# Decoder layer, fp32: inputs of the cross attention requested at the end of the self-attention block, and the first projection ahead of the key product

## The chip, the cores and the metric

The kernel runs on one core of a Trainium2 chip. The metric is the device time of one execution in microseconds; before the change the median of 3 runs is 1337.78 us (1329.46 to 1340.32). The engines are named as the profile names them: PE (TensorE, matmul; PEld its weight loads), DVE (VectorE), ACT (ScalarE), POOL (GpSimd) and SP (SyncE, which issues most DMAs here; SPq is its queue). Each runs its own instructions in program order and waits on semaphores.

## What is computed

One pre-norm decoder layer on `x` of 4 x 1024 x 256 in fp32: self-attention with rotary embedding (16 heads of 16), cross attention over 4 x 77 context rows (one head of 256), and a mixture of 8 experts in which each expert picks its 512 tokens. Cut to what matters:

```python
# self-attention
out = softmax(rot(q) @ rot(k).T * scale) @ v          # per batch and head
x = x + (out @ proj_w.T + proj_b)
# cross attention, k = v = ctx_1024
kp = ctx @ Wk.T ; vp = ctx @ Wv.T + bv
qp = layernorm(x) @ Wq.T + bq
x = x + softmax(qp @ kp.T / 16) @ vp @ Wo.T + bo
# experts: top-cap tokens of each expert, gelu between two layers, gated, scattered
x = x + moe(layernorm(x))
```

## The kernel before, in words

Four stages follow one another, each in a block of its own with a barrier of all engines between: `project_qkv`, `attend`, `cross_attend`, `experts`. A block's instructions on each engine stand in the order of the code; nothing reorders them.

`attend` runs over 4 batches (`bodies`: first and last written out, the middle ones a loop), 8 half groups each. Each half group ends in a tail that is spread over engines and lies behind in time: ACT copies the sum to `b_out` (L615), SP gathers the denominators into `b_sums` (`Tail.sums`, L432), DVE inverts them (`Tail.invert`, L438), SP stores and spreads the reciprocals (`Tail.spread`, L443 and L446), POOL scales into `b_att` (`Tail.scale`, L454), and SP stores that to `attended` in DRAM (`Tail.store`, L461). `ost` is that DRAM tensor, `s_os` the semaphores of its stores (`b_out_stored`). The very last half group's tail is done within `cross_attend`.

`cross_attend` works on 8 chunks of 512 tokens. For a chunk, SP loads the attention's output (`attT`, tile `c_attT`, 512 KB) and `x` (`xs`, tile `c_x`, 512 KB) in `load(j)`, alternating between two buffers; POOL adds the projection's bias (`bias`, L1043, to `c_xb`); PE multiplies with `wp` (`project(j)`); DVE adds both (`residual`, L1074) and makes mean and variance, ending in `c_nm` (L1132); ACT normalises (`c_xn`, L972); PE transposes (L1231) and multiplies with the folded keys `c_kqw`; softmax; a product with the folded values `c_vo`. Most PE products have one line, L1155, that of the helper `product`. The steps `s` overlap three chunks.

Ahead of the chunks stand products of the context `cT` (tile `c_ctxT`, 308 KB) alone: keys, values, keys folded with `wq`. Their results are taken by ACT (L967, L982). In the queues, at the start of the block: SP issues `cT`, `load(0)`, `load(1)` (five DMAs, 2356 KB), then the last group's `sums` and `spread`, the first expert's weights (2 MB), two constants, the last `store`, and then `load(2)` and on. PE does keys, `project(0)`, values, folded keys, `project(1)`. DVE sets constants, inverts the last sums, and then takes the residual of chunk 0. The buffers of all this are allocated at the block's start, in memory that `attend` has used.

`experts` has two buffers for an expert's output, `yb` (`e_yb`) and `y` (`e_y`).

Of the kernel before, what the change touches and what calls it, by code (L numbers as in the profile page):

```python
# [13 lines left out]
P = 128  # L14
B, L, C = 4, 1024, 256
T = B * L
H, D = 16, 16
SK = 77
E, FF = 8, 1024
CAP = T // E  # L20
KC = C // P
CH = 512
NT = CH // P
G = 4
# [437 lines left out]
                .then_inc(self.s_os[h], 16)  # L462


def attend(nc, ps, ident, group0, s_clear0, stores, last_stores, tail, cw, s_cw, wts, qst, kst, vst):

# [4 lines left out]
    with ctx:  # L471
# [87 lines left out]
        @block.sync  # L559
        def _(sp):  # L560
            def rows(g, h):
                for s, p in ((0, 0), (1, 0), (0, 1), (1, 1)):
                    m = NT * (2 * s + p)
                    for r in range(2):
                        at = HR * s + RS + r
                        sp.dma_start(qs[g][at:at + 1, p, CH * h:CH * h + CH].bitcast(F32),
                                     mT[m:m + NT, r, :].bitcast(F32)).then_inc(s_row[h], 16)

            def ones(g):
                sp.wait_ge(s_clear[g], 4)  # L570
# [12 lines left out]

            def body(i, first, last):
                n = before(i, first)
                for hg in range(NH):
                    back = not (first and hg == 0)
                    m, x = 8 * i + hg - 1, (hg - 1) % 2
                    if back:
                        tail.sums(sp, m, x)  # L590
                    if hg > 1:
                        tail.store(sp, m - 1, i, (hg - 2) // 2, 1 - x)
                    elif not first:
                        tail.store(sp, m - 1, i - 1, NG - 1, 1 - x)
                    if not (last and hg == NH - 1):

                        sp.wait_ge(s_ra, n["rows"] + hg + 1)
                        rows((hg + 1) // 2 % NG, (hg + 1) % 2)
                    if first and hg == 0:
                        last_stores(sp)  # L600
                    if back:
                        tail.spread(sp, m, x)
                    if first and hg == 2:
                        load_context_weights(sp, cw, s_cw, wts)
            bodies(sp, body)
            tail.store(sp, NH * B - 2, B - 1, NG - 1, 0)

        @block.scalar
# [229 lines left out]
            values(B - 1, KT * NH - 1, 1)  # L838


def cross_attend(nc, ps, ident, tail, cw, s_w, ew, s_ew, sums, s_sum, lg, x, ost, wts, out, xrow):

# [5 lines left out]
    with ctx:  # L848
# [6 lines left out]
        SW = SK + E  # L855
        SZ = SK + 2 * E
        ALLK = B * SK
        bqb = sb("c_bqb", [P, KC, P])
        ones = sb("c_ones", [P, P])
        cT = sb("c_ctxT", [P, KC, ALLK])  # L860
        kp = sb("c_kp", [P, KC, ALLK])
        vp = sb("c_vp", [P, KC, ALLK])
        voT = sb("c_voT", [P, KC, ALLK])
# [3 lines left out]
        csum = sb("c_wrn_sums", [P, E])  # L867
        vo = sb("c_vo", [SK, B, C])
        vw = sb("c_vw", [SK, B, E])
        xs = sb("c_x", [P, 2, NT, C])  # L870
        xb = sb("c_xb", [P, 2, NT, C])
        x1 = sb("c_x1", [P, 3, NT, C])
        x2 = sb("c_x2", [P, 2, NT, C])
        xn = sb("c_xn", [P, 2, NT, C])
        z = sb("c_z", [P, 2, NT, C])
        attT = sb("c_attT", [P, 2, KC, CH])
        xnT = sb("c_xnT", [P, KC, CH])
        pT = sb("c_probsT", [SK, CH])
        st = sb("c_st", [P, 2 * NT, 6])
# [14 lines left out]

        s_one = sem("c_ones_set")
        s_set = sem("c_constants_ready")
        s_cx = sem("c_ctx_in")
        s_at = two("c_att_in")
        s_xi = two("c_x_in")
        s_xb = sem("c_x_biased")  # L900
        s_kp, s_kpe = sem("c_k_product"), sem("c_k_taken")
        s_vp, s_vpe = sem("c_v_product"), sem("c_v_taken")
# [21 lines left out]
        def after(eng, s, n):  # L924

            if n > 0:
                eng.wait_ge(s, n)

        @block.sync
        def _(sp):  # L930
            def load(j):
                b, q = j // 2, j % 2
                after(sp, s_m1, 2 * j - 2)
                if j == J - 2:
                    for h in range(2):
                        sp.wait_ge(tail.s_os[h], 16 * G * B * NG)
                sp.dma_start(attT[:, q], ost[b][q].rearrange("k p n -> p k n")).then_inc(s_at[q], 16)
                after(sp, s_xb, j - 1)
                sp.dma_start(xs[:, q], x[b, q].rearrange("t p c -> p t c")).then_inc(s_xi[q], 16)

            sp.dma_start(cT[:], wts["ctxT"]).then_inc(s_cx, 16)
            load(0)
            load(1)
            tail.sums(sp, LAST, 1)
            tail.spread(sp, LAST, 1)
            load_expert(sp, ew, s_ew, wts, 0, 0)
            for n in range(2):
                sp.dma_start(sums[n][:], wts[("blk", "low")[n]]).then_inc(s_sum, 16)
            tail.store(sp, LAST, B - 1, NG - 1, 1)
            for s in range(NS + 1):  # L950
                if s + 2 < J:
                    load(s + 2)
                if 0 <= s - 2 < J:
                    j = s - 2
                    sp.wait_ge(s_m2e, 2 * j + 2)
                    sp.dma_start(out[j // 2, j % 2].rearrange("t p c -> p t c"), x2[:, j % 2]).then_inc(s_so[j % 2], 16)
                if 0 <= s - 3:
                    j = s - 3
                    sp.wait_ge(s_nb, j + 1)
# [190 lines left out]
        def _(pe):  # L1150
# [17 lines left out]
                        last.then_inc(s_m1, 1)  # L1168

            pe.wait_ge(s_w, 12 * 16)  # L1170
            pe.wait_ge(s_cx, 16)
            for e in range(KC):
                product(ps[:, e, 0:ALLK], [(wk[:, k, P * e:P * e + P], cT[:, k, :]) for k in range(KC)]).then_inc(s_kp, 1)
            project(0)
            for e in range(KC):
                product(ps[:, 2 + e, 0:ALLK], [(wv[:, k, P * e:P * e + P], cT[:, k, :]) for k in range(KC)])\
                    .then_inc(s_vp, 1)
# [75 lines left out]
                    project(s + 1)  # L1253


def experts(nc, ps, ident, ew, s_w, sums, s_in, lg, nw, xrow, wts, out):

# [6 lines left out]
    with ctx:  # L1264
# [67 lines left out]
        UP = (3, 4, 7)  # L1332
        NH = 4
        hf = sb("e_hT", [P, NH, CAP])
        yb = sb("e_yb", [P, CT, C])
        y = sb("e_y", [P, CT, C])

        s_z = sem("d_z_ready")
        s_ez = sem("d_exp_ready")
# [499 lines left out]
def program(nc, a, out):  # L1839
# [13 lines left out]
    with ExitStack() as ctx:  # L1853
        hold = lambda n, s, d=F32, c=ctx: c.enter_context(nc.sbuf_tensor(n, s, d))
        signal = lambda n: ctx.enter_context(nc.semaphore(n))
        ps = ctx.enter_context(nc.psum_tensor("banks", [P, 8, 512], F32))

        ident = hold("ident", [P, P])
        cw = {n: hold(f"c_{n}", shapes[n]) for n in CW}
        s_id, s_ld0, s_cw, s_sum = [signal(n) for n in ("ident_in", "group0_loaded", "c_weights_in", "sums_in")]  # L1860
        s_ew = {n: signal(f"e_{n}_in") for n in ("w1", "w2")}
        s_ew.update({n: [signal(f"e_{n}_in{x}") for x in range(2)] for n in ("b1", "b2")})
        tail = Tail(hold, signal, ost, dsum)
        with ExitStack() as early:
            group0 = (hold("b_q0", [P, 2, L], F32R, early), hold("b_k0", [P, 2, L], F32R, early),
                      hold("b_v0", [P, KT, G, VW], F32, early), s_ld0)
            s_clear0 = signal("group0_pad_cleared")
            stores = (hold("a_parts", [P, 4, 2, L], F32R, early), hold("a_v", [P, 2, NT, H, VW], F32, early),
                      [signal(f"a_v_stored{h}") for h in range(2)], [signal(f"a_qk_stored{h}") for h in range(2)])
            last_stores = project_qkv(nc, ps, ident, s_id, group0, s_clear0, stores, x5, a["wqkv"], a["bqkv"], a["cos"], a["sin"], a["ident"],  # L1870
                        qst, kst, vst)
            attend(nc, ps, ident, group0, s_clear0, stores, last_stores, tail, cw, s_cw, a, qst, kst, vst)
        lg = hold("logits", [P, T // P, E])
        sums = [hold(n, [P, P]) for n in ("same_expert", "same_expert_before")]
        ew = {"w1": hold("e_w1", [P, KC, FF]), "w2": hold("e_w2", [P, FF // P, C]),
              "b1": hold("e_b1", [P, 2, FF // P]), "b2": hold("e_b2", [P, 2, C])}
        cross_attend(nc, ps, ident, tail, cw, s_cw, ew, s_ew, sums, s_sum, lg, x5, ost, a, out5, xrow)
        experts(nc, ps, ident, ew, s_ew, sums, s_sum, lg, cw["nw"], xrow.rearrange("b h t p c -> (b h t p) c"), a, out)


# [39 lines left out]
```

## Time and profile before

| | |
|---|---|
| median of 3 runs | 1337.78 us (1329.46 to 1340.32) |
| the profiled execution | 1338.93 us, span 1337.2, mean granted clock 0.91 |
| PE busy | 1133.1 us (85%) |
| DVE busy | 1067.9 us (80%) |
| ACT busy | 762.6 us (57%) |
| POOL busy | 394.9 us (30%) |
| DMA | 120.40 MB, mean 90 GB/s |

The profile shows one execution. A timeline row gives start, duration, engine, line and operation with output<-input, how many such instructions are merged, and in brackets how long the engine sat idle before and what released it. The granted clock is that of TensorE, 1.00 being 2.4 GHz and 0.50 being 1.2 GHz. The cross attention lies between the barriers at about 885.5 and 1031.7 us.

### The profile page before, as it was taken

The page shows a single profiled execution, that of the slowest core. Times are in us where ns is not written, and L with a number is a line of the kernel's source. Part 1 is how long each engine was busy: PE and PEld are TensorE (multiplying, and loading weights), DVE is VectorE, ACT ScalarE, POOL GpSimd, SP SyncE. Part 2 cuts the span into 40 slices and gives each one's busy share as a digit, 9 for nine tenths or more (in the row PEclk, how much of TensorE's full clock was granted, in tenths as well). Part 3 has the DMA queues.
Part 4 walks back from the last instruction along what each step waited for, and adds up shares of the span by engine and source line. Part 5 has one row for each costly group of instructions (what it writes and reads, how often), then busy time and mean ns, then how long its engine had stood idle before and what let it go on. Part 6 is the DMA issues. An engine that isn't in the chain of part 4 may idle for free. (4 is left out here: it accounts for less than half of the span.)

```text
span 1337.2 us, 24904 instructions
## 1 busy us (share of the span) xinstructions
PE 1133.1 (85%) x8470; PEld 613.7 (46%) x8470; DVE 1067.9 (80%) x2458; ACT 762.6 (57%) x929; POOL 394.9 (30%) x396
## 2 busy tenths in 40 slices
PE   5776779899999999899999999988874027999994
PEld 3444433333333333333333333347764026878894
DVE  6776479799999999899999999626875977677751
ACT  2322105687778888778887888843553003466561
POOL 4665684202121121202212000022100021665663
PEclk9989767999999999999999999988885557999997
DMA  3344854644431344324433100035522011354332
GB/s 104 142 172 174 205 158 99 151 102 81 77 72 40 59 82 78 55 40 78 81 75 62 35 15 18 15 91 184 173 79 83 0 63 48 99 156 125 106 96 27
DMA packets 84105, 120.40 MB, mean 90 GB/s; under 512 B 23248, under 2 KB 57040, under 8 KB 82960
## 3 DMA queue, kind: packets, MB, share of 16 engines
q1 hardware_dynamic: 68000, 78.98, 19.6%
q0 software_dynamic: 15984, 39.86, 15.9%
q8 instruction: 69, 1.13, 0.4%
q14 instruction: 52, 0.43, 0.1%
HBM read 75.67 MB, written 42.21 MB: 88 GB/s over the span
## 5 line engine op out<-in xcount | busy, mean ns | idle before, releaser
L686 DVE TENSOR_REDUCE b_max_halves<-banks 128x1 f32<-128x512 f32 x1024 | 628.2, 680 | 27.3 <-PE banks L753 26.9
L628 ACT ACTIVATE b_probs<-banks 128x1024 f32<-128x1024 f32 x512 | 519.9, 1025 | 144.2 <-PE banks L805 142.7
L753 PE MATMUL banks<-b_k,b_q 62*128 62x512 f32 x1024 | 399.2, 472 | 4.8 <-DVE b_max L703 3.1
L805 PE MATMUL banks<-b_q,b_k 64*128 64x512 f32 x1024 | 388.4, 458 | 12.9 <-DMA b_q<-b_max_rows 6.5
L775 PE MATMUL banks<-b_probs,b_v 128*32 128x256 f32 (+1 forms) x3840 | 321.4, 407 | 2.3 <-ACT b_out L615 0.3
L805 PEld LDWEIGHTS banks<-b_q,b_k 64*128 64x128 f32 x1024 | 160.9, 186 | 229.7 <-issue 153.7
L753 PEld LDWEIGHTS banks<-b_k,b_q 62*128 62x128 f32 x1024 | 166.3, 191 | 38.3 <-DVE b_max_halves L686 33.2
L775 PEld LDWEIGHTS banks<-b_probs,b_v 128*32 128x32 f32 x3840 | 75.9, 108 | 166.0 <-issue 85.8
L454 POOL TENSOR_TENSOR b_att<-b_out,b_rec_spread 128x512 f32<-128x512 f32 x32 | 41.1, 1284 | 309.8 <-DMA b_rec_spread<-reciprocals 309.6
L386 POOL DMA_DIRECT2D b_q<-q_stacks x60 | 31.7, 531 | 252.4 <-PE banks L775 232.6
L337 PE MATMUL banks<-a_w,a_xnT 128*128 128x512 f32 x128 | 73.0, 700 | 37.5 <-DVE a_v L266 36.2
L1467 POOL DMA_INDIRECT e_x<-rows,d_idx x32 | 43.9, 1372 | 130.0 <-DVE d_wx L1648 66.2
L1440 ACT ACTIVATE e_hTh<-banks,e_b 128x512 fp32r<-128x512 f32 x64 | 44.1, 689 | 54.0 <-PE banks L1783 51.2
L1684 DVE TENSOR_TENSOR e_hTl<-e_hT,e_hTh 128x512 fp32r<-128x512 f32 x64 | 43.5, 689 | 38.5 <-ACT e_hT L1443 38.5
L1783 PE MATMUL banks<-e_w2h,e_hTh 128*128 128x256 f32 x256 | 73.9, 289 | 0.0
L1783 PE MATMUL banks<-e_w2l,e_hTh 128*128 128x256 f32 x256 | 73.1, 286 | 0.0
L1783 PE MATMUL banks<-e_w2h,e_hTl 128*128 128x256 f32 x256 | 73.1, 285 | 0.0
L314 POOL TENSOR_TENSOR a_t<-a_qk,a_sin 128x256 f32<-128x256 f32 x64 | 52.8, 845 | 66.6 <-DVE a_t L269 66.6
L1426 ACT ACTIVATE e_xTh<-banks 128x512 fp32r<-128x512 f32 x16 | 8.7, 595 | 98.5 <-PE banks L1771 98.5
L217 ACT ACTIVATE a_parts<-banks 128x512 fp32r<-128x512 f32 x32 | 18.9, 592 | 75.7 <-PE banks L350 72.4
L1783 PE MATMUL banks<-e_xTh,e_w1h 128*128 128x512 f32 x128 | 54.0, 422 | 2.6 <-DVE e_xTl L1661 2.6
L1486 POOL DMA_INDIRECT out_x<-e_y,d_idx x32 | 52.2, 1631 | 8.6 <-issue 7.3
(230 smaller groups left out, 1542.6 us busy)
## 6 DMA issues: line engine op xcount, KB each, us to landing
e_w<-in_w SPq DMA_DIRECT2D x16, 1024.0 KB, 10.2
v_tiles<-a_v SPq DMA_DIRECT2D x8, 1024.0 KB, 8.3
q_stacks<-a_parts SPq DMA_DIRECT2D x32, 256.0 KB
k_stacks<-a_parts SPq DMA_DIRECT2D x32, 256.0 KB
b_q<-q_stacks POOLq DMA_DIRECT2D x30, 256.0 KB, 6.5
b_k<-k_stacks POOLq DMA_DIRECT2D x30, 256.0 KB, 7.3
b_v<-v_tiles POOLq DMA_DIRECT2D x15, 512.0 KB, 9.2
a_x<-in_x SPq DMA_DIRECT2D x8, 512.0 KB, 5.9
```

The source lines that it names most:

```text
L314: ins = g.tensor_tensor(dst[:, :, :, u], src[:, :, :, 1 - u], ss, ALU.mult)
L337: mm(ps[:, 2 + q, :], xnT[:, c % 2, k, P * t:P * t + P], w[:, k, 0:2 * C], start=(k == 0), stop=(k == KC - 1))
L628: nc.scalar.activation(pr[:, S % NP, u], ps[:, 2 * u:2 * u + 2, :], ACT.Exp, scale=D ** -0.5).then_inc(s_ex[u], 1)
L686: v.tensor_reduce(mxp[:, (k // NB) % 2, s, p, t, kh:kh + 1], ps[:, bank(last), :], AX.X, ALU.max)\
L753: nc.tensor.matmul(ps[:, bank(last), :], qs[g][stack, p, at:at + P], ks[g][stack, p, CH * kh:CH * kh + CH], start=True, stop=True).then_in ...
L775: last = nc.tensor.matmul(ps[VW * j:VW * j + VW, PV, at], vs[hg // 2][:, kt, j, :], pr[:, S % NP, j // 2, j % 2, at], start=(kt == 0), sto ...
L805: return nc.tensor.matmul(ps[:, 2 * u + s, :], ks[g][stack, u, P * kt:P * kt + P], qs[g][stack, u, CH * h:CH * h + CH], start=True, stop=True)
L1440: nc.scalar.activation(hh[:, f, :], ps[:, UP[f % len(UP)], :], ACT.Gelu, bias=b1[:, x, f:f + 1])
L1467: g.indirect_dma_start(xe[:, x, h, :], None, xrow, bass.IndirectOffsetOnAxis(ap=idx[:, n, h:h + 1], axis=0)).then_inc(s_g[x], 16)
L1486: g.indirect_dma_start(out, bass.IndirectOffsetOnAxis(ap=idx[:, n, h:h + 1], axis=0), y[:, h, :], None, compute_op=ALU.add).then_inc(s_sc, 16)
L1684: v.tensor_tensor(hl[:, f, :], hf[:, f % NH, :], hh[:, f, :], ALU.subtract).then_inc(s_hl, 1)
L1783: ins = mm(o, a, b, start=(start and m == 0), stop=(stop and m == len(pairs) - 1))
```

## The change

The buffers `cT`, `attT` and `xs` and their semaphores move into a class `Firsts`, whose memory is kept from before the attention to the end. The five DMAs (context, chunks 0 and 1) are issued by SP at the end of `attend`, behind the last spread and ahead of the last store of that block, after a wait for batch 0's stores. In `cross_attend` PE does `project(0)` ahead of the keys' product and waits for the context between them. `experts` uses the two halves of `xs` as `yb` and `y`.

```diff
+class Firsts:
+    def __init__(self, sb, sem):
+        self.cT = sb("c_ctxT", [P, KC, B * SK])
+        self.attT = sb("c_attT", [P, 2, KC, CH])
+        self.xs = sb("c_x", [P, 2, NT, C])
+        self.s_cx = sem("c_ctx_in")
...
+    def att(self, sp, ost, j):
+        sp.dma_start(self.attT[:, j % 2], ost[j // 2][j % 2].rearrange("k p n -> p k n")).then_inc(self.s_at[j % 2], 16)
+    def rows(self, sp, x, j):
+        sp.dma_start(self.xs[:, j % 2], x[j // 2, j % 2].rearrange("t p c -> p t c")).then_inc(self.s_xi[j % 2], 16)
...
             bodies(sp, body)
+            for h in range(2):
+                sp.wait_ge(tail.s_os[h], 16 * G * NG)
+            sp.dma_start(firsts.cT[:], wts["ctxT"]).then_inc(firsts.s_cx, 16)
+            for j in range(2):
+                firsts.att(sp, ost, j)
+                firsts.rows(sp, x, j)
             tail.store(sp, NH * B - 2, B - 1, NG - 1, 0)
...
             def load(j):
-                b, q = j // 2, j % 2
-                after(sp, s_m1, 2 * j - 2)
+                sp.wait_ge(s_m1, 2 * j - 2)
                 if j == J - 2:
                     for h in range(2):
                         sp.wait_ge(tail.s_os[h], 16 * G * B * NG)
-                sp.dma_start(attT[:, q], ost[b][q].rearrange("k p n -> p k n")).then_inc(s_at[q], 16)
-                after(sp, s_xb, j - 1)
-                sp.dma_start(xs[:, q], x[b, q].rearrange("t p c -> p t c")).then_inc(s_xi[q], 16)
-
-            sp.dma_start(cT[:], wts["ctxT"]).then_inc(s_cx, 16)
-            load(0)
-            load(1)
+                firsts.att(sp, ost, j)
+                sp.wait_ge(s_xb, j - 1)
+                firsts.rows(sp, x, j)
+
             tail.sums(sp, LAST, 1)
...
             pe.wait_ge(s_w, 12 * 16)
+            project(0)
             pe.wait_ge(s_cx, 16)
             for e in range(KC):
                 product(ps[:, e, 0:ALLK], [(wk[:, k, P * e:P * e + P], cT[:, k, :]) for k in range(KC)]).then_inc(s_kp, 1)
-            project(0)
...
-        yb = sb("e_yb", [P, CT, C])
-        y = sb("e_y", [P, CT, C])
+        yb, y = pair[:, 0], pair[:, 1]
```

On SP, from the last spread of the attention on, the rows before are these (`b_att_ready` is POOL's scaling, the branches the change of block, L929 the start of `cross_attend`):

```order
L446 DMA b_rec_spread<-reciprocals 16x512 [waits b_rec_stored]
L446 DMA b_rec_spread<-reciprocals 16x512 x3
L461 DMA attended<-b_att 16x512 [waits b_att_ready]
L461 DMA attended<-b_att 16x512 x3
L471 UNCONDITIONAL_BRANCH
L929 UNCONDITIONAL_BRANCH [waits barrier_Pool_Activation_PE_DVE_SP_release]
L941 DMA c_ctxT<-in_ctxT 128x616
L937 DMA c_attT<-attended 128x2x512
L939 DMA c_x<-in_x 128x4x256
L937 DMA c_attT<-attended 128x2x512
L939 DMA c_x<-in_x 128x4x256
L432 DMA b_sums<-b_out 32x1x16 [waits b_out_taken]
```

And with the change (L626, L477 and L480 are the loads, L948 the start of `cross_attend`):

```order
L446 DMA b_rec_spread<-reciprocals 16x512 [waits b_rec_stored]
L446 DMA b_rec_spread<-reciprocals 16x512 x3
L626 DMA c_ctxT<-in_ctxT 128x616 [waits b_out_stored1,b_out_stored0]
L477 DMA c_attT<-attended 128x2x512
L480 DMA c_x<-in_x 128x4x256
L477 DMA c_attT<-attended 128x2x512
L480 DMA c_x<-in_x 128x4x256
L461 DMA attended<-b_att 16x512 [waits b_att_ready]
L461 DMA attended<-b_att 16x512 x3
L489 UNCONDITIONAL_BRANCH
L948 UNCONDITIONAL_BRANCH [waits barrier_Pool_Activation_PE_DVE_SP_release]
L432 DMA b_sums<-b_out 32x1x16 [waits b_out_taken]
```

The five loads have moved from behind the barrier to ahead of it and of the last store; `b_sums` is now the first DMA of the block. The 8 DMAs behind it keep their order.

On PE, at the start of `cross_attend`, before (two passes of fp32 appear as one instruction here and as two in the trace):

```order
L1149 UNCONDITIONAL_BRANCH [waits barrier_Pool_Activation_PE_DVE_SP_release]
L1155 MATMUL banks<-c_ctxT,c_wk 128x308 [waits c_ctx_in,c_weights_in]
L1155 MATMUL banks<-c_ctxT,c_wk 128x308 x3
L1155 MATMUL banks<-c_wp,c_attT 128x256 [waits c_att_in0]
L1155 MATMUL banks<-c_wp,c_attT 128x256 x7
L1155 MATMUL banks<-c_ctxT,c_wv 128x308 x4
L1155 MATMUL banks<-c_kp,c_wq 128x308 [waits c_k_taken]
```

With the change:

```order
L1164 UNCONDITIONAL_BRANCH [waits barrier_Pool_Activation_PE_DVE_SP_release]
L1170 MATMUL banks<-c_wp,c_attT 128x256 [waits c_att_in0,c_weights_in]
L1170 MATMUL banks<-c_wp,c_attT 128x256 x7
L1170 MATMUL banks<-c_ctxT,c_wk 128x308 [waits c_ctx_in]
L1170 MATMUL banks<-c_ctxT,c_wk 128x308 x3
L1170 MATMUL banks<-c_ctxT,c_wv 128x308 x4
L1170 MATMUL banks<-c_kp,c_wq 128x308 [waits c_k_taken]
```

The 8 products with `c_attT` have moved ahead of the 4 with `c_wk`; the rest stays.

## Rows read from the trace of the kernel before

**Rows 1.** Chain of waits in order of time, first piece: start us, us, what

```profile
1032.60 0.24 DVE d_io L1503
```

**Rows 2.** Timeline around the barrier, SP and ACT: start us, us, engine line op

```profile
875.47 1.70 SPq L446 DMA_DIRECT2D b_rec_spread<-reciprocals  x4
...
880.04 1.71 SPq L461 DMA_DIRECT2D attended<-b_att  x4
...
882.92 0.60 ACT L615 ACTIVATE b_out<-banks 128x512 f32<-128x512 f32 x1 [1.27 <-PE banks L775]
...
885.48 0.36 SPq L941 DMA_DIRECT2D c_ctxT<-in_ctxT  x1
...
887.94 2.86 SPq L432 DMA_DIRECT2D b_sums<-b_out  x4
```

**Rows 3.** Windows: length, busy us (x) of PE PEld DVE ACT POOL, clock, DMA share, GB/s

```profile
882.86:885.48 2.62, 0.00 (x1) 0.00 (x0) 0.00 (x0) 0.60 (x1) 0.00 (x0) 1.00 0.00 0
885.48:888.64 3.16, 0.00 (x0) 0.03 (x1) 1.25 (x8) 0.00 (x0) 0.21 (x1) 0.50 0.67 192
888.64:892.60 3.96, 3.96 (x9) 2.68 (x10) 0.00 (x0) 0.43 (x1) 0.42 (x1) 0.54 0.99 338
892.60:896.05 3.45, 3.45 (x17) 3.04 (x16) 0.00 (x0) 0.43 (x1) 1.94 (x1) 1.00 0.45 143
896.05:905.30 9.25, 9.25 (x41) 7.10 (x39) 6.91 (x25) 3.94 (x10) 3.63 (x2) 1.00 0.29 66
```

**Rows 4.** Timeline of the cross attention's start, all engines

```profile
888.64 4.12 PE L1155 MATMUL banks<-c_ctxT,c_wk 128*128 128x308 f32 x8 [5.78 <-DMA c_ctxT<-in_ctxT]
...
896.12 2.36 POOL L1043 TENSOR_TENSOR c_xb<-c_x,c_bp 128x1024 f32<-128x1024 f32 x1 [1.58 <-DMA c_x<-in_x]
...
896.94 0.25 DVE L438 RECIPROCAL b_rec<-b_sums 128x16 f32<-128x16 f32 x1 [10.01 <-DMA b_sums<-b_out]
...
897.11 1.22 DVE L1074 TENSOR_TENSOR c_x<-banks,c_xb 128x512 f32<-128x512 f32 x2
...
902.10 0.17 ACT L967 ACTIVATE c_wrn_sums<-banks 128x8 f32<-128x8 f32 x1
...
903.55 0.16 DVE L1132 SCALAR_TENSOR_TENSOR c_nm<-c_mv,c_rs 128x4 f32<-128x4 f32 x1
...
905.87 1.09 PE L1231 MATMUL banks<-ident,c_xn 128*128 128x128 f32 x8 [0.58 <-ACT c_xn L972]
```

**Rows 5.** Timeline of SP: last store of the attention, load of chunk 2

```profile
904.67 2.74 SPq L461 DMA_DIRECT2D attended<-b_att  x4
...
907.46 0.42 SPq L937 DMA_DIRECT2D c_attT<-attended  x1
```

**Rows 6.** Timeline of the step of chunks 1 and 2

```profile
915.35 2.35 POOL L1043 TENSOR_TENSOR c_xb<-c_x,c_bp 128x1024 f32<-128x1024 f32 x1 [11.86 <-DMA c_x<-in_x]
...
918.00 2.34 POOL L1043 TENSOR_TENSOR c_xb<-c_x,c_bp 128x1024 f32<-128x1024 f32 x1 [0.31 <-DMA c_x<-in_x]
...
918.14 2.23 DVE L67 TENSOR_TENSOR c_tm<-c_tm,c_rs 128x4 f32<-128x4 f32 x1
...
920.14 1.99 PE L1155 MATMUL banks<-c_vo,c_probsT 77*128 77x256 f32 x8 [0.68 <-ACT c_probsT L967]
...
920.79 2.08 ACT L972 ACTIVATE c_xn<-c_x,c_nm,c_rs 128x256 f32<-128x256 f32 x4 [0.70 <-DVE c_nm L1132]
...
922.92 1.92 PE L1231 MATMUL banks<-ident,c_xn 128*128 128x128 f32 x8 [0.79 <-ACT c_xn L972]
```

**Rows 7.** Window of the last steps, at the low clock

```profile
998.10:1031.76 33.66, 18.10 (x64) 15.48 (x64) 17.01 (x67) 11.36 (x25) 0.00 (x0) 0.50 0.23 79
```

**Rows 8.** Timeline of DVE, ends of three steps (`c_nm`)

```profile
988.50 0.17 DVE L1132 SCALAR_TENSOR_TENSOR c_nm<-c_mv,c_rs 128x8 f32<-128x8 f32 x1
...
999.94 0.17 DVE L1132 SCALAR_TENSOR_TENSOR c_nm<-c_mv,c_rs 128x8 f32<-128x8 f32 x1
...
1015.93 0.16 DVE L1132 SCALAR_TENSOR_TENSOR c_nm<-c_mv,c_rs 128x4 f32<-128x4 f32 x1
```

More of the change, by code:

```diff
@@ L462, in store, with attend @@
                 .then_inc(self.s_os[h], 16)
-def attend(nc, ps, ident, group0, s_clear0, stores, last_stores, tail, cw, s_cw, wts, qst, kst, vst):
+class Firsts:
[4 more added lines that the diff above has]
+        self.s_cx = sem("c_ctx_in")
+        self.s_at = [sem(f"c_att_in{n}") for n in range(2)]
+        self.s_xi = [sem(f"c_x_in{n}") for n in range(2)]
+    def att(self, sp, ost, j):
+        sp.dma_start(self.attT[:, j % 2], ost[j // 2][j % 2].rearrange("k p n -> p k n")).then_inc(self.s_at[j % 2], 16)
+    def rows(self, sp, x, j):
+        sp.dma_start(self.xs[:, j % 2], x[j // 2, j % 2].rearrange("t p c -> p t c")).then_inc(self.s_xi[j % 2], 16)
+def attend(nc, ps, ident, group0, s_clear0, stores, last_stores, tail, firsts, cw, s_cw, x, ost, wts, qst, kst, vst):
     ctx = ExitStack()
@@ L838, in _, with cross_attend @@
             values(B - 1, KT * NH - 1, 1)
-def cross_attend(nc, ps, ident, tail, cw, s_w, ew, s_ew, sums, s_sum, lg, x, ost, wts, out, xrow):
+def cross_attend(nc, ps, ident, tail, firsts, cw, s_w, ew, s_ew, sums, s_sum, lg, x, ost, wts, out, xrow):
     ctx = ExitStack()
@@ L857, in cross_attend @@
         ALLK = B * SK
+        cT, attT, xs, s_cx, s_at, s_xi = firsts.cT, firsts.attT, firsts.xs, firsts.s_cx, firsts.s_at, firsts.s_xi
         bqb = sb("c_bqb", [P, KC, P])
         ones = sb("c_ones", [P, P])
-        cT = sb("c_ctxT", [P, KC, ALLK])
         kp = sb("c_kp", [P, KC, ALLK])
@@ L869, in cross_attend @@
         vw = sb("c_vw", [SK, B, E])
-        xs = sb("c_x", [P, 2, NT, C])
         xb = sb("c_xb", [P, 2, NT, C])
@@ L875, in cross_attend @@
         z = sb("c_z", [P, 2, NT, C])
-        attT = sb("c_attT", [P, 2, KC, CH])
         xnT = sb("c_xnT", [P, KC, CH])
@@ L896, in cross_attend @@
         s_set = sem("c_constants_ready")
-        s_cx = sem("c_ctx_in")
-        s_at = two("c_att_in")
-        s_xi = two("c_x_in")
         s_xb = sem("c_x_biased")
@@ L1253, in _, with experts @@
                     project(s + 1)
-def experts(nc, ps, ident, ew, s_w, sums, s_in, lg, nw, xrow, wts, out):
+def experts(nc, ps, ident, ew, s_w, sums, s_in, lg, nw, pair, xrow, wts, out):
     ctx = ExitStack()
@@ L1863, in program @@
         tail = Tail(hold, signal, ost, dsum)
+        firsts = Firsts(hold, signal)
         with ExitStack() as early:
@@ L1871, in program @@
                         qst, kst, vst)
-            attend(nc, ps, ident, group0, s_clear0, stores, last_stores, tail, cw, s_cw, a, qst, kst, vst)
+            attend(nc, ps, ident, group0, s_clear0, stores, last_stores, tail, firsts, cw, s_cw, x5, ost, a, qst, kst, vst)
         lg = hold("logits", [P, T // P, E])
@@ L1876, in program @@
               "b1": hold("e_b1", [P, 2, FF // P]), "b2": hold("e_b2", [P, 2, C])}
-        cross_attend(nc, ps, ident, tail, cw, s_cw, ew, s_ew, sums, s_sum, lg, x5, ost, a, out5, xrow)
-        experts(nc, ps, ident, ew, s_ew, sums, s_sum, lg, cw["nw"], xrow.rearrange("b h t p c -> (b h t p) c"), a, out)
+        cross_attend(nc, ps, ident, tail, firsts, cw, s_cw, ew, s_ew, sums, s_sum, lg, x5, ost, a, out5, xrow)
+        experts(nc, ps, ident, ew, s_ew, sums, s_sum, lg, cw["nw"], firsts.xs, xrow.rearrange("b h t p c -> (b h t p) c"), a, out)
 def kernel(**inputs):
```

## The prediction

> **What bounds the kernel now.** I read the chain of waits first. It is followed back from the last instruction and begins at 1032.60 us [rows 1], in the experts' stage; the barrier ahead of that stage cuts it. So the chain says nothing of the cross attention, and what the change is worth must be read from that stage's own timeline. The stages are serial: a barrier at 885.48 us lets the cross attention begin, and the next stage begins when it is over. Whatever the cross attention gains up to its last step comes off the span one for one.
>
> Next the timeline around the barrier. ACT takes the last attention output at 882.92 to 883.52, the last work ahead of the barrier, and SP's first load is issued at 885.48 [rows 2]. The reader sees all inputs of the new stage being asked for only then: five loads, then the tiny `b_sums` transfers behind them at 887.94. TensorE waits 5.78 us with nothing to do (from 882.86) until `c_ctxT` lands at 888.64, the last of the five loads lets POOL begin only at 896.12, and the sums land at 896.94 [rows 4]. VectorE can't add its first residual before that, since `tail.invert` stands ahead of it in its queue.
>
> Last the windows. The granted clock fell to 0.50 (1.2 GHz) during that idle time, stayed there from 885.48 on, and rose to 1.00 (2.4 GHz) during the context's product: 3.96 us at a mean of 0.54 [rows 3]. From 888.64 to 905.30 TensorE is busy without a gap (3.96, 3.45 and 9.25 us, busy throughout) [rows 3]. Then it waits for `c_xn`, which ACT normalises in 2.08 us (as at 920.79 [rows 6]) after `c_nm` at 903.55, and the first transposes start at 905.87 [rows 4].
>
> **The change part by part.**
>
> *The five loads, from 885.48 to the end of the attention.* SP is free after the four `b_rec_spread` transfers (875.47 + 1.70 = 877.17). Its next instruction waits for POOL's `b_att` and is issued at 880.04 [rows 2]. The five issues took 887.94 - 885.48 = 2.46 us before, so they now run from about 877.25 to 879.7, inside that wait. The added wait on `b_out_stored` asks for batch 0 alone, which was stored hundreds of us before. Queued behind the five are only the four stores of `attended` and the barrier. The stores took 1.71 us; behind a full queue the like stores at 904.67 took 2.74 [rows 5]. Even so SP is done at 880.04 + 2.74 = 882.8, ahead of ACT's 883.52. Cost: nothing, with 0.7 us of cover. The last of five loads was usable 896.12 - 885.48 = 10.64 us after the first issue, so now at about 887.9, and the first projection's input, with 820 of the 2356 KB that the five move, at about 882 (an estimate by share of bytes, from the same 10.6 us).
>
> *The last group's sums.* They are now the first thing SP issues in the new stage: 885.5, and 2.86 us for four issues [rows 2]. They landed 0.8 us after the last load before; now the last load is there at 887.9, the last sum about 889. So `b_rec` comes near 889.1, not 896.94, and all that SP does behind it (spread, expert weights, the last store, the load of chunk 2) moves up by about 7.5 us. VectorE's residual is then held by the projection alone.
>
> *The order on TensorE.* `project(0)` goes ahead of the keys. Its data is there when the barrier opens, and I take 885.65 for its start, 0.17 us behind SP's first (an estimate; no row shows TensorE unhindered there). The gapless work until the first transposes stays the same: context 3.96 x 0.54 = 2.14 us at the full clock, then 3.45 and 9.25, together 14.84 us [rows 3]. What it loses in clock must be added. Before, the low level went on for about 3.6 us after TensorE had restarted (3.96 us at a mean of 0.54: 3.6 at 0.50 and the rest at 1.00). I take the same after the new restart: 3.6 us at half speed lose 1.8. So TensorE is through at 885.65 + 14.84 + 1.8 = 902.3. Bounds: no fall of the clock, 900.5; low until 892.1, when it rose before (888.64 + 3.6 rounded down), 903.7.
>
> *Are the transposes then held by something else?* `project(0)` ends at 885.65 + 3.45 + 1.8 = 890.9, the residual follows it, and residual to `c_nm` was 903.55 - 897.11 = 6.44 us: 897.3. ACT has its copies ahead of `c_xn` in its queue; the last ended at 902.27 [rows 4], with the second projection of 3.7 us still to run on TensorE until 905.30, so 3.0 us ahead of TensorE's end; now 899.3, and `c_xn` at 899.3 + 2.1 = 901.4. TensorE is the last at 902.3, by 0.9. POOL's two bias additions of 2.36 us now stand from 885.7 to 890.5, beside VectorE's constants; if they hold VectorE until 890.5, the residual still waits for nothing else. First transposes: 905.87 becomes 902.35, a **gain of 3.5 us**, of the 5.78 that TensorE waited. The rest of that wait is not given back, because the barrier's own 2.8 us remain and ACT's and TensorE's chain is dense.
>
> *Chunks 2 and 3.* Before, `attT` of chunk 2 was issued at 907.46, behind 2 MB of expert weights, and its `c_x` reached POOL at 915.35; POOL ran both bias additions from 915.35 to 920.34 [rows 5, 6]. Beside them VectorE's L67 on 128 x 4 numbers took 2.23 [rows 6], where `c_nm`, of the same size, took 0.16 [rows 4], and `c_nm` of chunk 1 waited for it; ACT began `c_xn` at 920.79 and the transposes waited until 922.92. Now the load is issued near 900 and lands near 907.5, so POOL is through by 912.3, in a time when VectorE waits for ACT's exponentials. `c_nm` comes 2 us earlier, but TensorE had its products with `c_vo` until 922.13 (920.14 + 1.99) [rows 6], so only about **0.7 us** reach the path. The Trainium skill (GPSIMD Engine Reference, 1. Specifications) says that GpSimd's memory interfaces are shared with VectorE, with contention for operations that have two inputs in SBUF; L67 is one, and the row agrees. By that rule alone 2 us would be gained; the sum goes by the rows of TensorE.
>
> *The experts' `e_yb` and `e_y`* lie in the memory of `c_x`, same shapes, freed long before: nothing. From step 2 on each chunk's loads are released by the projections, and the steps hang on one another through the engines.
>
> Sum: 3.5 + 0.7 = 4.2 us. The profiled execution took 1338.93 (span 1337.2 and 1.7 around it), so 1334.7; the median of the runs is 1337.78, 1.15 less, which gives **1333.6 us**.
>
> **Rivals.**
> - *The start stays fast* (no fall of the clock, as the gap is now about 2.8 us and not 5.78). For it: the clock was still at 1.00 for all of 882.86 to 885.48 [rows 3]. Against: it fell just there. Gain 5.3 + 0.7 = 6.0: 1331.8.
> - *The later clock.* The stage goes by the clock: the step from 988.50 to 999.94 took 11.4 us, the next, at 0.50, 16.0 with less work in it, and from 998.10 on all is at 0.50, with 18.10 us of TensorE work [rows 7, 8]. Shifting the stage's gaps by 4 us may move the falls. In favour: one or two steps fast that were slow, 4.5 to 9 us more, 1324.6 to 1329. Nothing in the trace says which way.
> - *The other side, by the same mechanism:* two more steps fall to the low level, 2 x 4.5 = 9 us lost against 4.2 gained: 1342.6, slower than before. It decides from one such step on.
> - *SP is held at the attention's end.* The four stores stand behind 2.36 MB. The Trainium skill (DMA: Bandwidth & Descriptors, Queues, rings and completion order) says that an engine's DMAs go through its own rings in order. If the stores' issue waited for the loads to drain, until 887.9, SP would reach the barrier at 889.6, and the stage would begin some 4.8 us later, all its inputs there: 1338.4. Against it: the stores at 904.67 lost only 1.0 us behind 2 MB [rows 5]; it decides when SP loses over 0.7 us, and cancels the gain from 4.9.
> - *The loads don't come early*, because they share the engines with the attention's last transfers: gain 1 to 2 us, 1336. Against: from 882.86 to the barrier nothing at all was moved [rows 3].
>
> **How the numbers follow.** As summed 0.50; fast start 0.12; later clock in favour 0.15; against 0.10; SP held 0.05; loads late 0.08. The prediction is the likeliest, 1333.6. The runs of before lie 10.9 us apart (1329.46 to 1340.32), so a median of some runs may be off by 3. The likeliest case alone reaches from 1330 to 1337; with the clock's cases the range is 1327 to 1340. About 1% (13 us) is what a measurement of this kernel can tell from no change: faster by more needs the best clock pattern and a low median, 0.08; slower by more 0.03; within 1% 0.89.
>
> **What the profile would show.** Right: the five loads issued from 877 to 880 and the barrier still at about 885.5 (relative to the last `b_out`); TensorE's first matmul with `c_wp` within 0.3 us of it, at clock 0.50 for 3 to 4 us; `b_rec` near 889; first transposes 3.5 us nearer to the barrier; POOL's bias additions for chunks 2 and 3 some 8 us earlier, and no 2 us operation on VectorE. Wrong: a barrier that comes later after ACT's last take; `b_rec` later than 891; the first transposes waiting for ACT; or steps of 14 to 16 us where there were 11.4, which would be the clock.

## The result

| | before | changed |
|---|---|---|
| median (runs) | 1334.55 us (20) | 1327.36 us (20) |
| lowest to highest | 1328.66 to 1344.09 | 1319.33 to 1332.55 |
| ratio | | 0.9942, 95% interval 0.9923 to 0.9961 |
| profiled execution, span | 1337.2 us | 1322.4 us |
| barrier to barrier, cross attention | 146.3 us | 133.3 us |
| experts | 305.4 us | 306.7 us |

The change makes the kernel faster by 0.58% (7.2 us by the medians; 0.39% to 0.77%), so within 1%, as forecast to be likeliest; the forecast size was 4.2 us. With more runs the median of before stands at 1334.55 and not 1337.78. The two profiled executions lie 14.8 us apart. That is more than the medians do: 3.1 us of it are ahead of the barrier (it came at 882.37 and not 885.48), where only the issue of the loads was added; in the profiles below the barrier came anywhere from 882.4 to 885.9, with and without that.

The end of the attention and the start of the cross attention in the changed kernel, from the timeline (as [rows 2, 4, 5]; L626, L477 and L480 are the loads, L1170 is the helper `product`, L1058 POOL's bias, L1089 the residual, L1147 `c_nm`, L1246 the transposes):

```profile
874.27 0.36 SPq L626 DMA_DIRECT2D c_ctxT<-in_ctxT  x1
...
876.22 0.47 SPq L480 DMA_DIRECT2D c_x<-in_x  x1
...
876.91 2.31 SPq L461 DMA_DIRECT2D attended<-b_att  x4
...
879.35 0.60 ACT L639 ACTIVATE b_out<-banks 128x512 f32<-128x512 f32 x1 [1.27 <-PE banks L799]
...
882.37 2.81 SPq L432 DMA_DIRECT2D b_sums<-b_out  x4
...
882.54 4.67 POOL L1058 TENSOR_TENSOR c_xb<-c_x,c_bp 128x1024 f32<-128x1024 f32 x2
...
882.56 5.09 PE L1170 MATMUL banks<-c_wp,c_attT 128*128 128x256 f32 x16 [3.26 <-PEq L489]
...
882.83 2.09 DVE L1075 TENSOR_SCALAR c_wrn<-c_wr,c_nw 128x8 f32<-128x8 f32 x1
...
884.84 2.40 DVE L1075 TENSOR_SCALAR c_wrn<-c_wr,c_nw 128x8 f32<-128x8 f32 x1
...
887.49 2.24 PE L1170 MATMUL banks<-c_ctxT,c_wk 128*128 128x308 f32 x8
...
887.89 0.25 DVE L438 RECIPROCAL b_rec<-b_sums 128x16 f32<-128x16 f32 x1
...
888.06 1.22 DVE L1089 TENSOR_TENSOR c_x<-banks,c_xb 128x512 f32<-128x512 f32 x2
...
894.62 0.17 DVE L1147 SCALAR_TENSOR_TENSOR c_nm<-c_mv,c_rs 128x4 f32<-128x4 f32 x1
...
895.67 2.07 ACT L987 ACTIVATE c_xn<-c_x,c_nm,c_rs 128x256 f32<-128x256 f32 x4
...
898.64 1.04 PE L1246 MATMUL banks<-ident,c_xn 128*128 128x128 f32 x8
...
898.82 0.43 SPq L477 DMA_DIRECT2D c_attT<-attended  x1
```

The five loads go out between 874.27 and 876.69, the barrier opens 2.42 us behind ACT's end (882.37 behind 879.95; before 1.97, and 1.84 to 2.52 in the profiles of all kernels below, with early loads or without), and TensorE starts 0.19 us behind it. `b_rec` is there 5.5 us behind the barrier (11.5 before), the first transposes come at 16.27 us (20.39 before). VectorE's two tiny constants (L1075) take 2.09 and 2.40 us instead of 0.22 beside POOL's bias additions; TensorE's own work still ended last ahead of the first transposes, which show no wait.

The windows of the two profiles, counted from the barrier, show what the prediction had left to chance: the clock of the later steps. In each pair the first window is 15 to 95 us behind the barrier, the second the rest of the stage; the columns are as in [rows 3]. The changed kernel:

```profile
897.37:977.37 80.00, 68.17 (x407) 57.22 (x405) 65.32 (x234) 39.80 (x90) 14.12 (x6) 0.98 0.47 160
977.37:1015.71 38.34, 20.11 (x80) 17.34 (x80) 20.71 (x89) 14.54 (x33) 0.00 (x1) 0.55 0.29 96
```

The same two of a second profile of the kernel before (e_before, below):

```profile
898.87:978.87 80.00, 69.45 (x356) 59.42 (x355) 60.99 (x204) 34.58 (x79) 15.41 (x7) 0.85 0.48 157
978.87:1029.54 50.67, 31.17 (x149) 26.72 (x148) 30.81 (x128) 22.17 (x49) 0.00 (x0) 0.67 0.28 94
```

The column to read is the clock: 0.98 against 0.85 in 80 us. The low level (0.50) held for 3 us in the one and for 24 us in the other ((1 - 0.85) / 0.5 x 80). "Fall" below is a change from 1.00 to 0.50.

### The profile page after: what moved, and what is told of

It is laid out like the page before. It is cut to its first block and busy times, and to the rows that moved or that the text cites. A ratio compares the mean times of both kernels' runs of the same rounds, so it can differ in the third digit from the quotient of the medians.

```text
span 1322.4 us, 24905 instructions
## 1 busy us (share of the span) xinstructions
PE 1129.7 (85%) x8470; PEld 608.6 (46%) x8470; DVE 1069.6 (81%) x2458; ACT 763.1 (58%) x929; POOL 394.5 (30%) x396
## 5 line engine op out<-in xcount | busy, mean ns | idle before, releaser
L829 PE MATMUL banks<-b_q,b_k 64*128 64x512 f32 x1024 | 389.0, 458 | 11.5 <-DMA b_q<-b_max_rows 5.1
L1500 POOL DMA_INDIRECT out_x<-c_x,d_idx x32 | 52.2, 1631 | 8.6 <-issue 7.3
```

Source lines behind the costliest of these rows:

```text
L829: return nc.tensor.matmul(ps[:, 2 * u + s, :], ks[g][stack, u, P * kt:P * kt + P], qs[g][stack, u, CH * h:CH * h + CH], start=True, stop=True)
L1500: g.indirect_dma_start(out, bass.IndirectOffsetOnAxis(ap=idx[:, n, h:h + 1], axis=0), y[:, h, :], None, compute_op=ALU.add).then_inc(s_sc, 16)
```

## The experiments

All ratios are to runs of the kernel before on the same chip, beside the variant's own; they needn't be the quotient of the two medians. In the table, "transposes" is the start of the first transposes of `c_xn` behind the barrier, "steps" the sum of the six distances between `c_nm` of chunk 1 and the sixth `c_nm` after it, "clock" the mean granted clock from 15 to 95 us, all from one profile each. A "filler" is a product whose result nobody uses.

| kernel | median us | ratio (95%) | stage | transposes | steps | clock |
|---|---|---|---|---|---|---|
| before (first profile) | 1334.55 | 1 | 146.3 | 20.4 | 79.3 | 0.85 |
| e_before | 1335.79 | 1.0000 (0.9972 to 1.0028) | 145.7 | 19.9 | 79.3 | 0.85 |
| changed | 1327.36 | 0.9942 (0.9923 to 0.9961) | 133.3 | 16.3 | 72.0 | 0.98 |
| e_after | 1329.59 | 0.9959 (0.9932 to 0.9986) | 131.6 | 17.9 | 71.6 | 1.00 |
| e_keep | 1334.29 | 0.9991 (0.9963 to 1.0019) | 140.5 | 19.5 | 74.9 | 0.91 |
| e_loads | 1327.95 | 0.9942 (0.9916 to 0.9968) | 133.4 | 16.4 | 72.5 | 0.98 |
| e_order | 1329.20 | 0.9957 (0.9933 to 0.9982) | 135.3 | 21.7 | 71.4 | 1.00 |
| e_order_plain | 1327.82 | 0.9951 (0.9927 to 0.9974) | 135.8 | 22.0 | 70.9 | 1.00 |
| e_sums_first | 1334.97 | 1.0004 (0.9977 to 1.0030) | 143.9 | 22.6 | 76.9 | 0.91 |
| e_shift1 | 1332.84 | 0.9981 (0.9954 to 1.0007) | 146.1 | 21.2 | 79.2 | 0.85 |
| e_shift3 | 1335.99 | 1.0020 (0.9995 to 1.0045) | 138.1 | 22.6 | 71.6 | 1.00 |
| e_tail | 1324.38 | 0.9940 (0.9916 to 0.9965) | 134.8 | 16.6 | 77.5 | 0.89 |
| e_warm_before | 1320.76 | 0.9921 (0.9894 to 0.9947) | 130.2 | 20.9 | 69.5 | 1.00 |
| e_warm_order | 1324.02 | 0.9919 (0.9888 to 0.9950) | 132.6 | 22.0 | 70.6 | 1.00 |
| e_warm_after | 1317.96 | 0.9881 (0.9851 to 0.9910) | 125.4 | 16.4 | 71.1 | 1.00 |
| e_warm_loads | 1316.60 | 0.9859 (0.9828 to 0.9890) | 125.7 | 16.5 | 71.3 | 1.00 |
| e_best | 1317.04 | 0.9873 (0.9843 to 0.9903) | 125.3 | 16.4 | 71.0 | 1.00 |

**The change taken apart.** e_after is the changed kernel itself; e_keep undoes both moves and leaves the buffers; e_loads and e_order each undo one.

> The changed kernel again, beside the variants. Its stage (from the barrier to the next one) was 133.3 us against 146.3 before; 4.1 us of that stood at the first transposes, 5.0 at the second, and the other 8 came later, in steps of 11.4 to 12.7 us where there were 12.7 to 14.1. Theory A (a mechanical gain of about 5 us; the rest is the clock's pattern of that one execution): ratio to before 0.994 to 0.997, first transposes again 16.3 us behind the barrier, while the low-clock time ahead of the last 32 us of the stage differs from the 7.8 us of the first profile. Theory B (the change itself keeps the later clock up): the stage is again about 133 us, with under 12 us of low clock ahead of its last 32 us.

> The changed kernel with both moves undone: the loads are issued at the start of the cross attention and the keys' product comes first; only the buffers kept across the stages and the experts' two outputs in the memory of c_x remain. Theory A: no different from before, ratio 0.998 to 1.002, first transposes about 20.4 us behind the barrier, b_rec 11.5 us behind it. Rival C (part of the gain is the placing of the buffers): faster than before by 2 us or more, ratio under 0.9985, in the experts' stage or from step 2 on.

e_loads, the early loads with the old order on TensorE:

```diff
             pe.wait_ge(s_w, 12 * 16)
-            project(0)
             pe.wait_ge(s_cx, 16)
             for e in range(KC):
                 product(ps[:, e, 0:ALLK], ...).then_inc(s_kp, 1)
+            project(0)
```

> The changed kernel with the keys' product ahead of the first projection, as before: the early loads alone. Theory A: TensorE starts at the barrier in either order and does the same work, so first transposes at 16.3 to 16.8 us and a time within 1 us of the changed kernel (ratio to before 0.994 to 0.997). Rival D (the order matters): the first residual is 2 us later, ACT's normalising ends the wait, and over 1.5 us of the gain are lost.

e_order, the loads back in the cross attention (e_keep has both edits):

```diff
-            for h in range(2):
-                sp.wait_ge(tail.s_os[h], 16 * G * NG)
-            sp.dma_start(firsts.cT[:], wts["ctxT"]).then_inc(firsts.s_cx, 16)
-            for j in range(2):
-                firsts.att(sp, ost, j)
-                firsts.rows(sp, x, j)
...
+            sp.dma_start(cT[:], wts["ctxT"]).then_inc(s_cx, 16)
+            for j in range(2):
+                firsts.att(sp, ost, j)
+                firsts.rows(sp, x, j)
             tail.sums(sp, LAST, 1)
```

> The changed kernel with the five loads issued at the start of the cross attention, as before, and the first projection ahead of the keys: the order alone. Theory A: TensorE waits for 820 KB and not for 308, starts 1.5 to 2.5 us later than before, and first transposes come at about 22 us; time 1 to 2 us above before (ratio 1.000 to 1.002). Rival D: the earlier residual brings 1 to 2 us (ratio 0.9985 to 0.9995).

Rival C falls: the placing of the buffers is worth nothing that can be measured (0.9991, 0.9963 to 1.0019). Theory A holds for the loads: with the old order their first transposes come at 16.4 us, as with the new one, and rival D falls. But it is wrong of the order. Alone it was expected 1 to 2 us slower, and its start is slower (transposes at 21.7), yet the kernel gains 0.43%. The profile has the gain in the steps, 71.4 us for six instead of 74.9 to 79.3, at a clock of 1.00. Theory B gets support: the changed kernel's later steps have the high clock in both of its profiles, and so has e_loads without the order (0.98). But e_keep, whose order of instructions is that of before, shows 0.91 and not 0.85, so one profile of a kernel is a weak witness of its clock.

**The clock held up by fillers.** To have the clock alike in all, products whose results nobody uses are put where TensorE waits for the softmax:

```diff
+            def warm(n):
+                for _ in range(n):
+                    mm(ps[:, 6, 384:512], ident[:], ident[:], start=True, stop=True)
             for s in range(NS):
                 if 0 <= s - 2 < J:
+                    after(pe, s_sce, s - 1)
+                    warm(3 if s < J else 14)
                     pe.wait_ge(s_pn, s - 1)
```

> The kernel before with filler products on TensorE while it waits for the softmax: three of 128 columns (about 0.5 to 0.9 us) ahead of the transposes of c_probs in steps with a projection, fourteen in the last two steps, into unused columns of a bank. Their results are not used. Theory A (what the change brings beyond 5 us is fewer falls of the clock in the later steps): the fillers close most of the waits of 1.6 us ahead of which the clock fell, low-clock time ahead of the last 32 us of the stage goes below 12 us from 32, the steps after the third are 11.4 to 12.3 us, and the kernel gains 5 us or more of its own, 1 to 4 more from the last two steps. Theory B (the falls don't come from these waits): the clock falls as before, and the fillers cost 0 to 4 us.

> The changed kernel with the same fillers. Theory A: with the clock alike in both, its distance to the filled kernel before is the mechanical gain alone, 4 to 5 us; the gain over the plain changed kernel is smaller than the fillers bring to the kernel before. Theory B: the distance stays 7 us or more.

The windows of the filled kernel before, and of the filled changed kernel:

```profile
897.43:977.43 80.00, 70.88 (x440) 61.03 (x439) 65.25 (x241) 40.15 (x92) 15.40 (x7) 1.00 0.51 171
977.43:1012.64 35.21, 21.68 (x159) 19.41 (x158) 24.11 (x97) 16.90 (x37) 0.00 (x1) 0.86 0.31 105
```

```profile
900.42:980.42 80.00, 71.35 (x454) 61.91 (x452) 65.63 (x245) 41.24 (x94) 14.10 (x6) 1.00 0.47 164
980.42:1010.80 30.38, 17.25 (x129) 15.56 (x128) 19.41 (x79) 13.27 (x30) 0.00 (x1) 0.85 0.32 107
```

Both stand at 1.00 for the 80 us and at 0.86 and 0.85 after, where before stood at 0.67. The kernel before gains 0.79% (0.53% to 1.06%) from fillers alone. The edit only adds work and a wait, and what the profile shows in return is the clock, so the low level in this stage costs the kernel before some 10 us on the mean (7 to 14 by the interval). Its 6 runs lie within 5.1 us (1319.79 to 1324.91), where the 20 of the plain one spread over 15; six runs spread less than twenty, and the 6 of e_warm_after spread over 8.0.

The first transposes of the filled kernel before, and of the filled changed kernel:

```profile
903.29 1.09 PE L1238 MATMUL banks<-ident,c_xn 128*128 128x128 f32 x8 [0.62 <-ACT c_xn L972]
```

```profile
901.85 1.04 PE L1253 MATMUL banks<-ident,c_xn 128*128 128x128 f32 x8
```

The profiled stages of the two differ by 130.21 - 125.38 = 4.8 us, of which 4.4 stand at these first transposes (20.86 and 16.43 us behind the barrier). **That is the mechanical gain**, what the change brings at an equal clock, and theory A's 4 to 5. The times agree with it but do not fix its size: the ratios differ by 0.9921 - 0.9881 = 0.0040, 5.3 us of 1334, the means of the same runs by 4.7 us (1321.65 and 1316.98) and their medians by 2.8, with six runs each and intervals that overlap.

e_warm_loads and e_warm_order take that gain apart:

> The early loads alone with the fillers. If the loads are the whole mechanical gain: stage 125.0 to 126.5 us, ratio 0.987 to 0.990, no different from the filled changed kernel. If the order has a share: over 1 us longer than that one.

> The order alone (loads late) with the fillers in all steps, so that the clock is alike. Theory A: against the filled kernel before (ratio 0.9921) it is 1 to 2 us slower, ratio 0.992 to 0.994, stage 131 to 132.5 us against 130.2. Rival G: it keeps its 5 us and comes to 0.988 to 0.990.

All of it is the loads'. The filled early loads alone (stage 125.7) are no different from the filled change (125.4), and with the fillers the order alone has nothing left: ratio 0.9919 beside 0.9921, a stage 2.4 us longer. So far as six runs can tell, what it gained in the plain kernel was clock.

**Does the order keep the clock up, or chance?** Two kernels shift the later steps without the order, by six or thirteen fillers ahead of the first transposes:

```diff
                     if j == 0:
                         pe.wait_ge(s_kqe, KC + 1)
+                        warm(6)
```

> The kernel before with six filler products (about 1.3 us) on TensorE ahead of the first transposes, and nothing else: all later steps stand 1.3 us later in the stage, as they do with the order alone. Theory F (the later steps' waits lie otherwise against the moments at which the clock is decided, and that shift gives the order alone its gain): faster than before although it only adds work, ratio 0.995 to 0.998, with one fall or none between 15 and 95 us of the stage. Rival G (the order of the products itself keeps the clock up): 1 to 2 us slower, ratio 1.000 to 1.002, with two or three falls.

> The same with thirteen fillers, about 2.9 us. Theory F: a time that does not follow the added work; somewhere between 4 us faster and 5 us slower than before, with another set of falls. Rival G: 2.5 to 3.5 us slower than before.

> The order alone again, now in the kernel before with its own buffers (no memory kept across the stages). Rival G (the order of the products keeps the clock up): ratio 0.994 to 0.997 as with the kept buffers (0.9957), at most one fall between 15 and 95 us of the stage. Theory H (the 5 us of the order alone were a matter of where the clock's moments lay in those executions): ratio 0.998 to 1.002, with one to three falls.

> The kernel before, unchanged, for a second look into its stage. Ratio 0.998 to 1.002. If falls in the later steps are the rule for it, two or three between 15 and 95 us of the stage, 20 us or more of low clock ahead of its last 32 us; if they are chance, another number than the three of the first profile.

The order's gain came again with the old buffers (0.9951; it was 0.9957 with the kept ones). The first row is the start of e_order_plain, where TensorE waits 7.10 us for the attention's output instead of 5.78 for the context; the second its 80 us:

```profile
888.24 6.59 PE L1155 MATMUL banks<-c_wp,c_attT 128*128 128x256 f32 x16 [7.10 <-DMA c_attT<-attended]
```

```profile
898.78:978.78 80.00, 68.61 (x409) 57.30 (x407) 63.34 (x233) 40.17 (x92) 15.39 (x7) 1.00 0.52 170
```

The second profile of before repeats the first nearly to the tenth: six steps in 79.3 us, clock 0.85. With two gains of the order that stand clear of 1, over 12 runs each, theory H (chance) falls for that gain.

The granted clock of every run, averaged over its whole span, says more than one profile each. Over the 98 runs of before that stood beside the experiments it goes with the time (correlation -0.81): the fastest quarter had 0.913 and 1329.8 us on the mean, the slowest 0.904 and 1339.6. By kernel, the mean is 0.909 for before, e_keep and e_sums_first, 0.913 for the changed kernel's 20 runs, 0.912 for e_after's 12 and 0.9125 for e_loads, and 0.914 and 0.913 for the order alone (e_order and e_order_plain). Up to a third of the changed kernel's rise is its shorter low stretch at the start. And the profiled executions are no fair sample: the two of the changed kernel (1324.07, 1323.94) lie 3.3 and 5.7 us below the medians of their kernels' runs, those of before (1338.93, 1337.31) 4.4 and 1.5 above. Their 3 and 0 us of low clock against 24 overstate the difference.

Theory F (a mere shift by 1.3 us does it) is left open. The profile of e_shift1 shows 0.85 again, and the interval of its 0.9981 includes 1. But over the runs the clock rose with the shifts too, to 0.912 (e_shift1) and 0.911 (e_shift3) from 0.9085 beside them, and e_shift1 was not slower for its added work. The profile of e_shift3 (1.00) is that of its shortest run; its 1.0020 includes 1. What in the order keeps the clock from falling stays open as well. Of the 17 falls between 15 and 95 us in all profiles, 14 came on the heels of two waits of TensorE close together, one of 1.0 to 1.8 us for the probabilities and one of 0.7 us for their transposes; yet in e_after and e_order the same two (1.4 to 1.5 and 0.7 us) passed without a fall. The last two steps have a wait of 3.6 to 3.9 us each, and there it fell in every kernel without fillers in those steps.

**The sums.** e_sums_first issues them ahead of the loads, in the kernel before:

```diff
+            tail.sums(sp, LAST, 1)
             sp.dma_start(cT[:], wts["ctxT"]).then_inc(s_cx, 16)
             load(0)
             load(1)
-            tail.sums(sp, LAST, 1)
```

> The kernel before with one move: the last group's sums are issued ahead of the five loads, all still in the cross attention. b_rec then comes at about 4 us behind the barrier, not 11.5, and the chain behind it on SP (expert weights, chunk 2) is earlier by up to 5 us, with the loads 2.9 us later. Theory A: TensorE's first product waits for the context 2.9 us longer, so first transposes at 22.5 to 23.5 us against 20.4; 1 to 3 us slower than before unless the clock gives some back. Rival E (the sums were what held the start): faster than before by 2 us or more.

Its start, from the timeline:

```profile
885.84 0.22 DVE L1060 TENSOR_SCALAR c_wrn<-c_wr,c_nw 128x8 f32<-128x8 f32 x1
...
888.97 0.25 DVE L438 RECIPROCAL b_rec<-b_sums 128x16 f32<-128x16 f32 x1 [2.16 <-DMA b_sums<-b_out]
...
891.18 4.40 PE L1155 MATMUL banks<-c_ctxT,c_wk 128*128 128x308 f32 x8 [8.77 <-DMA c_ctxT<-in_ctxT]
...
897.41 0.69 DVE L1074 TENSOR_TENSOR c_x<-banks,c_xb 128x512 f32<-128x512 f32 x1 [8.19 <-PE banks L1155]
```

`b_rec` is there 3.6 us behind the barrier, the context at 5.8, and the residual waits for TensorE (8.19 us). The first transposes come at 22.6 us as expected. Rival E falls: the sums alone did not hold the start. The time is that of before; the 2.2 us lost at the first transposes can't be told in it.

**Towards a better version.** e_tail has the fourteen fillers in the last two steps of the changed kernel alone; e_best has all fillers and three more behind the attention's last product.

> The changed kernel with the fourteen fillers in the last two steps alone, where TensorE waits 3.6 to 3.9 us for the softmax and its clock then stays low. If the fillers keep the clock up, the two steps of 16.0 and about 14 us lose 3 to 4 us each: 4 to 8 us faster than the changed kernel. If the clock falls all the same, no gain, and up to 2 us lost to the fillers.

> The changed kernel with the fillers in all steps and three more at the attention's end, where TensorE is done 0.6 us ahead of ACT. If they keep the clock up over the barrier, the first projection takes 3.5 us and not 5.1 and the first transposes come at 14.8 us: 1 to 2 us faster than the filled changed kernel (0.9881). If the clock falls all the same: the same time within 1 us.

e_tail's last two steps took 14.4 and 8.1 us in the profile, where the changed kernel's took 16.0 and 10.2, but the clock had fallen for 13.7 us in the middle of the stage. The ratio, 0.9940, is that of the changed kernel: the 4 to 8 us expected did not come. In e_best the clock fell at the barrier all the same, and the first projection took 5.17 us:

```profile
881.37 0.94 PE L864 MATMUL banks<-ident 128*128 128x128 f32 x6
...
884.60 5.17 PE L1172 MATMUL banks<-c_wp,c_attT 128*128 128x256 f32 x16 [2.30 <-PEq L489]
```

The filled versions of the change (e_warm_after, e_best, e_warm_loads) lie 1.2% to 1.4% below the kernel before, with intervals that end at 0.991 or below, and are faster than both kernels by their medians; their intervals all lie below that of the changed kernel (0.9923 to 0.9961).

## Why the prediction was right or wrong

- *Barrier and queue*: right. SP issued the five loads inside its wait for `b_att`, 0.22 us of that wait were left (876.69 to 876.91), and the stores took 2.31 us; SP was done at 879.22, ahead of ACT's 879.95. The rival in which SP is held falls, and so does the one of late loads. (The 4.8 us of the first did not follow from its rows: 889.6 - 883.52 is 6.1. And by its share of bytes the first projection's input was due at 881, not 882. Neither bears on the sum.)
- *Sums*: `b_rec` was put at 889.1, 3.6 us behind the barrier, and came 5.5 us behind it. It wasn't the sums: VectorE's constants, slowed beside POOL's bias additions, ran until 887.85. The prediction had allowed for that (until 890.5), and the residual at 888.06 was early enough. SP's chain moved up by 5.5 us against the barrier (the load of chunk 2 at 16.45 us, not 21.98), forecast 7.5.
- *First transposes*: 3.5 us forecast (16.9 us behind the barrier), 4.1 measured in the changed kernel (16.27) and 4.4 in the filled pair. The clock's fall cost 5.09 - 3.45 = 1.6 us, forecast 1.8. The rival of a fast start fell in all profiles, even with TensorE busy until 2.1 us ahead of the barrier (e_best). In e_after the low level lasted 6.2 us behind the barrier, and the transposes came at 17.9: the second bound of the estimate (903.7, so 18.2) does occur.
- *Chunks 2 and 3*: 0.7 us forecast; the second transposes came 32.45 us behind the barrier instead of 37.44, so 0.9 beyond the 4.1. But POOL didn't get through ahead of the softmax. The addition for chunk 3 still lay over `c_probs`, which took 1.66 us:

```profile
906.12 2.35 POOL L1058 TENSOR_TENSOR c_xb<-c_x,c_bp 128x1024 f32<-128x1024 f32 x1 [11.55 <-DMA c_x<-in_x]
...
908.75 2.36 POOL L1058 TENSOR_TENSOR c_xb<-c_x,c_bp 128x1024 f32<-128x1024 f32 x1 [0.28 <-DMA c_x<-in_x]
...
909.78 1.66 DVE L1105 TENSOR_TENSOR c_probs<-c_exp,c_rec 128x308 f32<-128x308 f32 x1
...
914.82 1.09 PE L1246 MATMUL banks<-ident,c_xn 128*128 128x128 f32 x8
```

  VectorE was held once more, only earlier in its queue. TensorE's chain ended the wait all the same.
- *The sum* was 4.2 us for what the filled pair shows as 4.8 in its stage (2.8 to 5.3 in its times): right in its mechanism and near in its size.
- **The step that failed** is the one on the later clock. The sum gave it nothing ("Nothing in the trace says which way"), and the likeliest case, at 0.50, was that the pattern of falls stays as it was; the favourable pattern had 0.15. The pattern did not stay. Before had 24 us of low clock between 15 and 95 us in both its profiles, the changed kernel 3 and 0; the six steps took 79.3 us and then 72.0. Over all runs it was less: the gain of 7.2 us is 2.4 more than the mechanical 4.8, and the mean clock of the runs rose from 0.909 to 0.913. That split is not sharp, as the interval of the gain is 5.2 to 10.3 us and the 4.8 come from one pair of profiles; that the clock has a share shows best in the order alone, which has no mechanical gain and still brought 0.43% and 0.49%. Treating the clock as a shift of unknown sign was wrong in a second way: the trace of before came from an execution above the median (1338.93 against 1334.55), with TensorE at the low level for 24 of 80 us, from which most disturbances lead upward. Of the eight edited kernels without fillers in the steps (the changed one, e_keep, e_loads, both of the order, e_sums_first, both shifts) only e_shift1 showed as low a clock in its profile, and none a lower one. Why an edit moves the falls stays open.

## What to carry to other kernels

Inputs of a stage that exist earlier should be asked for inside a wait of the issuing queue ahead of the barrier; here that alone made the filled stage 4.5 us shorter (130.2 to 125.7), of the 5.8 that TensorE had stood still, and the order of the products had no mechanical gain. Where a stage runs with the clock now low, now high, measure it also with fillers that hold the clock: the profiled stages can then be compared step by step, and they show whether a gain is the edit's own or the clock's. Look at the granted clock of all runs too, since the one that was profiled may lie some us above or below their median. And fillers can be an edit of their own: alone they gained 0.79% here, at least as much as the change (0.58%; the intervals overlap), and with the change 1.2% to 1.4%.

## What the runs showed of the hardware

- Three filler products per step (three took 0.94 us in e_best), and fourteen in each of the last two steps, went with a granted clock of 1.00 for 80 us in which it was 0.85 to 1.00 without them; the kernel before took 0.79% less time with them. In the last steps the clock still fell, 102 to 123 us behind the barrier in the five filled kernels.
- In all 17 profiles the clock fell to 0.50 between 0.7 us ahead of and 0.8 us behind the barrier, 1.9 to 3.3 us after TensorE's last product; work that began 0.2 us behind the barrier didn't prevent it, nor did three fillers that ended 2.1 us ahead of it.
- Beside POOL's 2.36 us additions on two inputs from memory, a VectorE operation on 128 x 8 numbers took 2.09 and 2.40 us instead of 0.22, and one on 128 x 308 took 1.66 instead of 0.48. The residual, which reads one input from PSUM, took its usual 1.22 us for two beside them (897.11 in the kernel before, [rows 4]). The Trainium skill (GPSIMD Engine Reference, 1. Specifications) names contention between the two engines for operations with two inputs in SBUF or in a faster two-port mode. The rows agree for the one on 128 x 308, which has two such inputs, and for the residual; the one on 128 x 8 takes one tile and a number per partition, and no row shows in which mode it ran.
